# Down-weight chunk transfers of a cross-attention and FFN kernel moved from SyncE's to ScalarE's instruction stream

## The chip, the core and the metric

One core of one Trainium2 chip runs the whole program. The metric is the device time of one launch in microseconds, the median of 3 runs. TensorE (PE) multiplies, VectorE (DVE), ScalarE (ACT) and GpSimd (POOL) work on elements, and SyncE (SP) computes nothing: before the change it issues every transfer of the kernel.

## The reference

```python
x = x + xattn(layernorm(x), ctx, Wq, Wk, Wv, Wo)      # 32 heads, 4 key/value heads, head size 128
h = layernorm(x)                                       # 8 x 112 rows of 1024
hid = relu(h @ up_w) ** 2                              # 1024 -> 2048
shared = hid @ down_w                                  # 2048 -> 1024
routed = ((h @ fc1_w) @ expert_w * sum(top2(h @ gate_w))) @ fc2_w
x = x + layernorm(shared + routed, gamma, beta)
```

Everything is float32. The change touches only how parts of `down_w` are prepared while `h @ up_w` is computed.

## The kernel before

**Arithmetic.** The matrix products are done with seven block products in place of eight (Strassen's scheme in Winograd's form), so sums of weight blocks are needed beside the blocks. Every float32 operand is split into a rounded part ("hi", written by ACT with a copy) and the rest ("lo", a subtraction on POOL or DVE), and each product is three matmuls (L2289, L2290, L2291: hi*hi, lo*hi, hi*lo).

**The up stage.** `h @ up_w` runs over 8 pairs of 128-column blocks of the weights, `p` = 0 to 7, and in each pair over 7 products, `n` = 0 to 6. A unit is one product, `u = 7 * p + n`, written here (p,n). One unit is 4 steps of 3 matmuls over 448 rows. Between the units of pair 0 TensorE also does the last 7 routed products. For each pair four weight blocks of 128x512 (called A11, A21, A22, A12, 256 KB each, in `slab_raw`) are loaded by `load_up` (L926). POOL makes four sums of them (`up_sum`, L1186; the first needs A21 and A22, and overwrites A21), and for n = 0, 1, 2, 3 and 6 the lo parts (`up_lo`, L1195), in the order sum 1, lo 0, sum 2, lo 1, lo 2, sum 3, sum 4, lo 3, lo 6. ACT makes all the hi parts (`up_hi`, L1524), DVE the lo parts for n = 4 and 5 (L2094). DVE combines each product into the running sums (`up_combine`, L2087), and ACT takes the finished block through Relu (L1535) and Square (L1537) into the hidden rows (`hidden_block`, for n = 2, 4, 5, 6). At n = 0 ACT copies the first product out of its bank (L1613).

**The chunks.** The down products, which come after the up stage, need sums of blocks of `down_w` too. They are made ahead of time in 16 chunks, c0 to c15. Each chunk is two loads of 256 KB (`load_chunk`, L940), four subtractions of 128x256 on DVE (`down_sums`, L2105), and one store of 512 KB to a scratch tensor in DRAM (`store_chunk`, L945). Four buffers are used: X and Z in `act_region_unrounded`, Y in `tile_region`, V in `small_region_unrounded`. The table `CHUNKS` says in which unit DVE makes the sums and in which buffer. c0 to c15 have their sums in (1,0) Y, (1,1) X, (1,3) Z, (1,4) V, (1,6) Y, (2,0) X, (2,3) Z, (2,4) V, (2,6) X, (3,0) Y, (3,3) Z, (3,5) X, (3,6) Y, (4,4) X, (4,6) Y and (5,5) Y.

**What sets the order of the transfers.** SP's list is written out by hand, unit by unit. In units n = 2, 3, 4 and 5 of each pair it waits until A11, A21, A22 or A12 of this pair has been used up and loads the block of the next pair: A11 behind POOL's lo 3, A21 behind DVE's lo part for n = 4, A22 behind DVE's lo part for n = 5, A12 behind POOL's lo 6. In unit (0,4) it loads c0 and in (0,5) c1 to c3. After that the rule is: two units behind the sums of a chunk comes its store (behind a wait for the fourth sum), and five units behind them the load of the next chunk in the same buffer (behind a wait for the store to have landed):

```python
for c in range(len(CHUNKS)):
    if CHUNK_UNIT[c] + 2 == u:
        store_chunk(c)
    later = [i for i in range(c + 1, len(CHUNKS)) if CHUNK_BUF[i] == CHUNK_BUF[c]][:1]
    if CHUNK_UNIT[c] + 5 == u:
        for i in later:
            load_chunk(i)
```

So c4 is loaded in (1,5) for its sums in (1,6), c5 in (1,6) for (2,0), c8 in (2,5) for (2,6), c11 in (3,4) for (3,5), c12 in (3,5) for (3,6), c13 in (4,3) for (4,4).

**ACT's list in the up stage** goes by the same units. In unit u it waits for the product and copies it if n = 0, then makes the hi part of unit u + 3 (in pair 0: u + 2, and two of them, (1,0) and (1,1), in (0,5)), and then does the hidden block, if the unit has one. The hi part of (p+1,1) thus comes in unit (p,5), in front of that unit's Relu, and it waits for POOL's sum 2 of pair p+1.

Of the kernel before, what the change touches and what calls it, by code (L numbers as in the profile page):

```python
# [11 lines left out]
P = 128  # L12
B, SQ, HID = 8, 112, 1024
SC = 375
NH, NKV, D = 32, 4, 128
# [197 lines left out]
def xattn_ffn(nc, x, ctxT, slabs, wkv, gate, gamma, beta, out):  # L213
    with ExitStack() as top:
# [440 lines left out]
        def _(sp):  # L655
# [272 lines left out]
            def down_base(kh):  # L928
                return slab_no(P_FFN) + NK + 2 * NK * kh

            def load_chunk(c):


                buf, use, m, kp = CHUNK_BUF[c], CHUNK_USE[c], c % 4, c // 4
                if use:
                    sp.wait_ge(s_cst[buf], 16 * use)
                to = CHUNK[buf].rearrange("p (e k c) -> p e k c", e=2, k=2)
                for kh in range(2):
                    blocks = slabs[down_base(kh):down_base(kh) + NK].rearrange("(e m) p c -> p e m c", e=2)
                    sp.dma_start(to[:, :, kh, :], blocks[:, :, m, 2 * P * kp:2 * P * (kp + 1)]).then_inc(s_cld[buf], 16)  # L940

            def store_chunk(c):
                buf, use, m, kp = CHUNK_BUF[c], CHUNK_USE[c], c % 4, c // 4
                sp.wait_ge(s_csum[buf], 4 * (use + 1))
                sp.dma_start(td_d[:, kp, :, m, :].rearrange("t p c -> p t c"),  # L945
                             CHUNK[buf].rearrange("p (t c) -> p t c", t=4)).then_inc(s_cst[buf], 16)

            def load_down(d):

                if d >= 2:  # L950
# [11 lines left out]
            for p in range(F_PAIRS):  # L962
                more = p + 1 < F_PAIRS
                for n in range(7):
                    u = 7 * p + n
                    if more and n == 2:
                        sp.wait_ge(s_ulo, lo_count(p, 3))
                        load_up(p + 1, "A11")
                    if more and n == 3:
                        sp.wait_ge(s_ulo2, 2 * p + 1)  # L970
                        load_up(p + 1, "A21")
                    if more and n == 4:
                        sp.wait_ge(s_ulo2, 2 * p + 2)
                        load_up(p + 1, "A22")
                    if more and n == 5:
                        sp.wait_ge(s_ulo, lo_count(p, 6))
                        load_up(p + 1, "A12")
                    if p == 0 and n == 4:
                        sp.wait_ge(s_ftlo, 4)
                        load_chunk(0)  # L980
                    if p == 0 and n == 5:
                        sp.wait_ge(s_mm, C_FFN + RT)
                        for c in range(1, 4):
                            load_chunk(c)
                    for c in range(len(CHUNKS)):
                        if CHUNK_UNIT[c] + 2 == u:
                            store_chunk(c)
                        later = [i for i in range(c + 1, len(CHUNKS)) if CHUNK_BUF[i] == CHUNK_BUF[c]][:1]
                        if CHUNK_UNIT[c] + 5 == u:
                            for i in later:  # L990
                                load_chunk(i)
            sp.wait_ge(s_ulo, lo_count(F_PAIRS - 1, 3))
            sp.wait_ge(s_ulo2, 2 * F_PAIRS - 1)
            load_down(0)
# [229 lines left out]
        def _(act):  # L1224
# [301 lines left out]
            def hidden_block(p, n, i):  # L1526
# [9 lines left out]
                act.wait_ge(s_relu, 4 * p + i + 1)  # L1536
                act.activation(to, to, ACT.Square).then_inc(s_sq, 1)  # L1537

            def down_hi(d):

                act.wait_ge(s_draw[d % 2], 16 * (d // 2 + 1))
                if d == 0:
                    act.wait_ge(s_up, UNITS - 3)
                elif d < 3:
                    act.wait_ge(s_up, UNITS - 2)
                elif d == 3:
                    act.wait_ge(s_up, UNITS)
                elif d == 24:
                    act.wait_ge(s_olo, 4 * 6)
                else:  # L1550
                    act.wait_ge(s_dmm, slab_done(d - 4 if d < 24 else d - 5))
                act.activation(d_slot(d)[0], RAWS[d % 2], ACT.Copy).then_inc(s_dhi, 1)
# [54 lines left out]
            for p in range(F_PAIRS):  # L1607
                last = p == F_PAIRS - 1
                for n in range(7):
                    u = 7 * p + n  # L1610
                    if n == 0:
                        act.wait_ge(s_up, u + 1)
                        act.activation(F_FIRST, UB[0][:, 0:HALF], ACT.Copy).then_inc(s_first_p, 1)  # L1613
                    for v in (u + 2,) if u < 5 else (7, 8) if u == 5 else (u + 3,):
                        if v < UNITS:
                            up_hi(v // 7, v % 7)
                    if p == 0 and n == 2:
                        act.wait_ge(s_mm, C_FFN + 4)
                        row_block_hi("T4", 9)
                    if last and n == 5:  # L1620
                        chunk_hi(0, 0)
                        chunk_hi(0, 1)
                    if n in F_TILES:
                        hidden_block(p, n, list(F_TILES).index(n))
                    if last and n == 5:
                        down_hi(0)
# [1166 lines left out]
```

## Time and profile before

| what | value |
|---|---|
| time, median of 3 runs | 1735.61 us (1735.61 to 1735.88) |
| the profiled execution, its own time | 1735.55 us |
| its span in the trace | 1733.8 us |
| granted TensorE clock, mean | 0.998 |
| TensorE matmul busy | 1705.7 us, 98% of the span |
| VectorE, ScalarE, GpSimd busy | 1026.1, 736.5, 961.6 us |
| up stage with chunk work (about) | 1440 to 1560 us from the span's start |

Times in the rows are microseconds from the span's start. SPq is SP's list of transfers: its durations are those of issuing, not of moving the data. A bracket at the end of a row says how long the engine had been idle before it, and what released it.

### The profile page before, as it was taken

The page shows a single profiled execution, that of the slowest core. Times are in us where ns is not written, and L with a number is a line of the kernel's source. Part 1 is how long each engine was busy: PE and PEld are TensorE (multiplying, and loading weights), DVE is VectorE, ACT ScalarE, POOL GpSimd, SP SyncE. Part 2 cuts the span into 40 slices and gives each one's busy share as a digit, 9 for nine tenths or more (in the row PEclk, how much of TensorE's full clock was granted, in tenths as well). Part 3 has the DMA queues.
Part 4 walks back from the last instruction along what each step waited for, and adds up shares of the span by engine and source line. Part 5 has one row for each costly group of instructions (what it writes and reads, how often), then busy time and mean ns, then how long its engine had stood idle before and what let it go on. Part 6 is the DMA issues. An engine that isn't in the chain of part 4 may idle for free.

```text
span 1733.8 us, 24758 instructions
## 1 busy us (share of the span) xinstructions
PE 1705.7 (98%) x8539; PEld 1502.7 (87%) x8539; DVE 1026.1 (59%) x1520; ACT 736.5 (42%) x1409; POOL 961.6 (55%) x775
## 2 busy tenths in 40 slices
PE   9999999999999999999999999999999999889998
PEld 8988998899999988888988898889888987777887
DVE  3711112743434458875877577757657366866998
ACT  3311212233434357734773477247513224445342
POOL 2365553445555549875767576736534244555565
PEclk9999999999999999999999999999999999999999
DMA  8788876566677669834763476334223105643344
GB/s 271 227 285 284 295 246 214 171 195 219 207 225 247 218 208 303 290 121 142 249 219 121 149 243 211 116 102 152 82 81 113 55 31 175 220 147 97 133 145 158
DMA packets 214295, 319.37 MB, mean 184 GB/s; under 512 B 20304, under 2 KB 174416, under 8 KB 213328
## 3 DMA queue, kind: packets, MB, share of 16 engines
q1 hardware_dynamic: 214224, 318.49, 56.6%
q8 instruction: 37, 0.61, 0.1%
q14 instruction: 34, 0.28, 0.1%
HBM read 211.78 MB, written 106.66 MB: 184 GB/s over the span
## 4 chain that ended last, share of the span: by engine, by line
PE 90%; DVE 3%; POOL 3%; DMA 2%; issue 1%; ACT 1%; SPq 0%; DVEq 0%; POOLq 0%; ACTq 0%
PE bank L2289 28%; PE bank L2290 28%; PE bank L2291 28%; PE bank L2513 5%; POOL slab_raw L1186 1%; DMA slab_raw<-in_slabs 1%; PE bank L2375 1%; POOL tile_region_rounded L1195 1%; DVE act_region_unrounded L2105 1%; POOL act_region L1195 0%; DMA mid_region<-k_latents_scratch 0%; DVE tile_region L2105 0%; PE bank L2654 0%; PE bank L2361 0%; DVE slab_split_unrounded L2125 0%
## 5 line engine op out<-in xcount | busy, mean ns | idle before, releaser
L1102 POOL TENSOR_TENSOR tile_region<-tile_region,small 128x487 f32<-128x487 f32 x224 | 221.1, 1024 | 73.2 <-DVE small L1787 73.1
L2289 PE MATMUL bank<-mid_region 125*128 125x448 f32 (+4 forms) x608 | 248.3, 408 | 0.5 <-DMA mid_region<-k_latents_scratch 0.3
L2290 PE MATMUL bank<-mid_region 125*128 125x448 f32 (+4 forms) x608 | 229.4, 377 | 0.0
L2291 PE MATMUL bank<-mid_region 128*128 128x488 f32 (+4 forms) x572 | 215.0, 376 | 0.0
L2289 PE MATMUL bank<-mid_region,act_region 128*125 128x512 f32 (+3 forms) x434 | 168.5, 388 | 1.7 <-POOL act_region L1195 1.7
L2290 PE MATMUL bank<-mid_region,act_region 128*125 128x512 f32 (+3 forms) x434 | 168.3, 388 | 0.0
L1372 ACT ACTIVATE tile_region<-bank,small 128x487 f32<-128x487 f32 x224 | 153.8, 687 | 30.3 <-DVE small L1791 30.3
L1068 POOL TENSOR_TENSOR slab_raw<-slab_raw 128x256 f32<-128x256 f32 x128 | 98.4, 771 | 120.0 <-DMA slab_raw<-in_slabs 112.5
L1404 ACT ACTIVATE mid_region<-bank 125x512 fp32r<-125x512 f32 x224 | 136.7, 613 | 54.7 <-PE bank L2513 54.7
L1791 DVE TENSOR_REDUCE small<-bank 128x1 f32<-128x487 f32 x224 | 146.0, 653 | 20.8 <-PE bank L2291 20.8
L1842 DVE TENSOR_TENSOR mid_region<-bank,mid_region 125x512 fp32r<-125x512 f32 x224 | 151.8, 683 | 9.3 <-ACT mid_region L1404 9.3
L2291 PE MATMUL bank<-mid_region,act_region 128*125 128x512 f32 (+3 forms) x404 | 156.3, 387 | 0.0
L2513 PEld LDWEIGHTS bank<-ident,tile_region 128*125 128x125 f32 x896 | 131.4, 187 | 15.5 <-POOL tile_region L1102 1.6
L1086 POOL TENSOR_TENSOR slab_split<-slab_raw,slab_split 128x512 fp32r<-128x512 f32 x64 | 87.6, 1371 | 94.3 <-ACT slab_split L1322 94.2
L2513 PE MATMUL bank<-ident,tile_region 128*125 128x128 f32 x896 | 134.4, 273 | 0.8 <-DVE mid_region L1842 0.8
L2291 PE MATMUL bank<-act_region,mid_region 128*128 128x376 f32 (+3 forms) x366 | 128.5, 351 | 0.0
L2289 PEld LDWEIGHTS bank<-mid_region 128*128 128x128 f32 (+2 forms) x608 | 114.7, 189 | 13.8 <-issue 2.7
L2290 PEld LDWEIGHTS bank<-mid_region 128*128 128x128 f32 (+2 forms) x608 | 115.4, 190 | 9.6
L2291 PEld LDWEIGHTS bank<-mid_region 128*128 128x128 f32 (+2 forms) x572 | 107.5, 188 | 14.9
L1662 DVE TENSOR_TENSOR small_region<-bank,small_region 128x375 fp32r<-128x375 f32 (+1 forms) x40 | 22.4, 563 | 164.7 <-ACT small_region L1238 164.6
L1923 DVE TENSOR_TENSOR y_region<-y_region,bank 128x512 f32<-128x512 f32 x105 | 68.8, 682 | 83.0 <-PE bank L2291 82.2
L2289 PE MATMUL bank<-act_region,mid_region 128*128 128x376 f32 (+3 forms) x330 | 115.0, 348 | 0.0
(310 smaller groups left out, 4290.7 us busy)
## 6 DMA issues: line engine op xcount, KB each, us to landing
slab_raw<-in_slabs SPq DMA_DIRECT2D x112, 256.0 KB, 3.8
q_scratch<-y_region SPq DMA_DIRECT2D x16, 1792.0 KB, 8.1
mid_region<-q_scratch SPq DMA_DIRECT2D x32, 896.0 KB, 7.1
slab_raw<-in_slabs SPq DMA_DIRECT2D x48, 512.0 KB, 3.5
weight_sums_scratch<-slab_raw SPq DMA_DIRECT2D x32, 512.0 KB, 4.4
small_region_unrounded<-in_slabs SPq DMA_DIRECT2D x52, 256.0 KB, 4.8
v_scratch<-slab_split SPq DMA_DIRECT2D x8, 1536.0 KB, 7.7
slab_raw<-weight_sums_scratch SPq DMA_DIRECT2D x48, 256.0 KB, 4.5
```

The costliest lines, as they stand in the source:

```text
L1068: pool.tensor_tensor(out, a, b, op).then_inc(s_sum[h], 1)
L1086: pool.tensor_tensor(WB[n][1], WRAW[n], f32(WB[n][0]), ALU.subtract).then_inc(s_blo, 1)
L1102: pool.tensor_tensor(PR[i][:, 0:KEYS], PR[i][:, 0:KEYS], rrow[:, i:i + 1].broadcast_to([P, KEYS]), ALU.mult).then_inc(s_pn, 1)
L1372: act.activation(PR[i][:, 0:KEYS], SB[RING[i]][:, 0:KEYS], ACT.Exp, bias=negmax[:, i:i + 1], accum_out=rowsum[:, i:i + 1]).then_inc(s_exp, 1)
L1404: act.activation(PT[0][0:KT, :, i * P:(i + 1) * P], TB[RING[i]][0:KT, :].rearrange("p (t n) -> p t n", t=4), ACT.Copy).then_inc(s_pth, 1)
L1791: dve.reduce_max(negmax[:, i:i + 1], SB[RING[i]][:, 0:KEYS], AX.X, negate=True).then_inc(s_max, 1)
L1842: dve.tensor_tensor(PT[1][0:KT, :, cols], TB[RING[i]][0:KT, :].rearrange("p (t n) -> p t n", t=4), f32(PT[0][0:KT, :, cols]), ALU.subtract ...
L1923: return dve.tensor_tensor(Y[:, r, cols_of(eh)], Y[:, r, cols_of(eh)], GB[i][:, :], op)
L2289: pe.matmul(out_ap, w[0], a[0], start=first, stop=False)
L2290: pe.matmul(out_ap, w[1], a[0], start=False, stop=False)
L2291: return pe.matmul(out_ap, w[0], a[1], start=False, stop=last)
L2513: last = pe.transpose(TB[RING[i]][0:KT, t * P:(t + 1) * P], PR[i][:, t * KT:(t + 1) * KT], ident[:, :])
```

## The change

`load_chunk` and `store_chunk` move, with their waits, from SP's list to ACT's, and so 32 loads and 16 stores are issued by ACT. They stand in the same units, in ACT's list behind the unit's hi part and ahead of its hidden block. Sizes, buffers, semaphores and the order of the chunks stay. SP keeps `load_up` and everything else. `chunk_base` gives the same number as `down_base`.

```diff
 # SP's list
-                    if p == 0 and n == 4:
-                        sp.wait_ge(s_ftlo, 4)
-                        load_chunk(0)
-                    if p == 0 and n == 5:
-                        sp.wait_ge(s_mm, C_FFN + RT)
-                        for c in range(1, 4):
-                            load_chunk(c)
-                    for c in range(len(CHUNKS)):
-                        if CHUNK_UNIT[c] + 2 == u:
-                            store_chunk(c)
-                        later = [i for i in range(c + 1, len(CHUNKS)) if CHUNK_BUF[i] == CHUNK_BUF[c]][:1]
-                        if CHUNK_UNIT[c] + 5 == u:
-                            for i in later:
-                                load_chunk(i)
 # ACT's list
+            def load_chunk(c):
+                buf, use, m, kp = CHUNK_BUF[c], CHUNK_USE[c], c % 4, c // 4
+                if use:
+                    act.wait_ge(s_cst[buf], 16 * use)
+                to = CHUNK[buf].rearrange("p (e k c) -> p e k c", e=2, k=2)
+                for kh in range(2):
+                    blocks = slabs[chunk_base(kh):chunk_base(kh) + NK].rearrange("(e m) p c -> p e m c", e=2)
+                    act.dma_start(to[:, :, kh, :], blocks[:, :, m, 2 * P * kp:2 * P * (kp + 1)]).then_inc(s_cld[buf], 16)
+            def store_chunk(c):
+                buf, use, m, kp = CHUNK_BUF[c], CHUNK_USE[c], c % 4, c // 4
+                act.wait_ge(s_csum[buf], 4 * (use + 1))
+                act.dma_start(td_d[:, kp, :, m, :].rearrange("t p c -> p t c"),
+                             CHUNK[buf].rearrange("p (t c) -> p t c", t=4)).then_inc(s_cst[buf], 16)
...
                     for v in (u + 2,) if u < 5 else (7, 8) if u == 5 else (u + 3,):
                         if v < UNITS:
                             up_hi(v // 7, v % 7)
                     if p == 0 and n == 2:
                         act.wait_ge(s_mm, C_FFN + 4)
                         row_block_hi("T4", 9)
+                    if p == 0 and n == 4:
+                        act.wait_ge(s_ftlo, 4)
+                        load_chunk(0)
+                    if p == 0 and n == 5:
+                        act.wait_ge(s_mm, C_FFN + RT)
+                        for c in range(1, 4):
+                            load_chunk(c)
+                    for c in range(len(CHUNKS)):
+                        if CHUNK_UNIT[c] + 2 == u:
+                            store_chunk(c)
+                        later = [i for i in range(c + 1, len(CHUNKS)) if CHUNK_BUF[i] == CHUNK_BUF[c]][:1]
+                        if CHUNK_UNIT[c] + 5 == u:
+                            for i in later:
+                                load_chunk(i)
...
                     if n in F_TILES:
                         hidden_block(p, n, list(F_TILES).index(n))
```

## Rows read from the trace of the kernel before

**Rows 1.** The page's first part: busy time, share of the span and instructions.

```profile
PE 1705.7 (98%) x8539; PEld 1502.7 (87%) x8539; DVE 1026.1 (59%) x1520; ACT 736.5 (42%) x1409; POOL 961.6 (55%) x775
```

**Rows 2.** Busy time by stretch: us, PE, PEld, DVE, ACT, POOL, PEclk, DMA share, GB/s.

```profile
1404.00:1440.00 36.00, 36.00 (x166) 30.95 (x166) 20.76 (x21) 8.73 (x12) 12.92 (x8) 1.00 0.09 27
1440.00:1560.00 120.00, 105.48 (x502) 92.78 (x501) 90.41 (x117) 52.88 (x95) 71.02 (x54) 1.00 0.60 189
1560.00:1580.00 20.00, 20.00 (x99) 18.16 (x99) 7.10 (x11) 9.79 (x17) 12.91 (x10) 1.00 0.17 55
```

**Rows 3.** The chain that ended last, 1440 to 1557: start us, us, what.

```profile
1480.48 5.80 DMA slab_raw<-in_slabs
1520.53 5.65 DMA slab_raw<-in_slabs
1540.67 3.83 DMA slab_raw<-in_slabs
```

**Rows 4.** Who waited for what, POOL, 1440 to 1560: us, times, longest.

```profile
POOL slab_raw L1186 <- DMA slab_raw<-in_slabs: 10.9, 5, 3.4
```

**Rows 5.** L926 (`load_up`) by source, 1430 to 1560: issue ns min/median/max; landing.

```profile
L926 SPq DMA_DIRECT2D slab_raw<-in_slabs x26: 327/341/698, 1430.3 to 1558.9; - x26
...
DMA to landing us min/median/max: 2.4/3.2/6.4
```

**Rows 6.** SP's timeline: start us, us, what it issued.

```profile
1441.87 1.90 SPq L940 DMA_DIRECT2D act_region_unrounded<-in_slabs  x4
1443.82 0.98 SPq L940 DMA_DIRECT2D small_region_unrounded<-in_slabs  x2
...
1477.86 0.94 SPq L940 DMA_DIRECT2D small_region_unrounded<-in_slabs  x2
1478.85 0.47 SPq L945 DMA_DIRECT2D down_weight_sums_scratch<-act_region_unrounded  x1
1479.36 1.82 SPq L926 DMA_DIRECT2D slab_raw<-in_slabs  x2
```

**Rows 7.** ACT's timeline in units (0,5), (0,6), (1,5), (1,6) and (2,5).

```profile
1447.77 0.63 ACT L1524 ACTIVATE tile_region_rounded<-slab_raw 128x512 fp32r<-128x512 f32 x1 [2.77 <-POOL slab_raw L1186]
1448.31 0.56 ACT L1535 ACTIVATE slab_split_unrounded<-tile_region 128x448 f32<-128x448 f32 x1
...
1449.39 0.61 ACT L1524 ACTIVATE act_region<-slab_raw 128x512 fp32r<-128x512 f32 x1
...
1468.58 0.63 ACT L1524 ACTIVATE act_region<-slab_raw 128x512 fp32r<-128x512 f32 x1 [3.90 <-POOL slab_raw L1186]
...
1470.48 0.61 ACT L1524 ACTIVATE slab_split<-slab_raw 128x512 fp32r<-128x512 f32 x1
...
1490.44 0.63 ACT L1524 ACTIVATE slab_split<-slab_raw 128x512 fp32r<-128x512 f32 x1 [4.97 <-POOL slab_raw L1186]
```

**Rows 8.** POOL's timeline: lo (1,2), then sum 1 of pair 2, which waits for A22.

```profile
1450.08 1.31 POOL L1195 TENSOR_TENSOR act_region<-slab_raw,act_region 128x512 fp32r<-128x512 f32 x1 [0.31 <-ACT act_region L1524]
...
1464.41 1.29 POOL L1186 TENSOR_TENSOR slab_raw<-slab_raw 128x512 f32<-128x512 f32 x1 [2.23 <-DMA slab_raw<-in_slabs]
```

**Rows 9.** TensorE's timeline: the first matmul of (1,3), which waited for lo (1,3).

```profile
1456.31 0.47 PE L2289 MATMUL bank<-act_region,slab_split 128*128 128x448 f32 x1 [1.20 <-POOL tile_region_rounded L1195]
```

**Rows 10.** DVE's timeline: combine (0,6), sums of c3, c4 and c8.

```profile
1448.90 0.62 DVE L2087 TENSOR_TENSOR tile_region<-y_region,bank 128x448 f32<-128x448 f32 x1 [3.92 <-ACT slab_split_unrounded L1535]
...
1464.09 4.73 DVE L2105 TENSOR_TENSOR small_region_unrounded<-small_region_unrounded 128x256 f32<-128x256 f32 x4
...
1470.54 3.75 DVE L2105 TENSOR_TENSOR tile_region<-tile_region 128x256 f32<-128x256 f32 x4
...
1492.11 5.07 DVE L2105 TENSOR_TENSOR act_region_unrounded<-act_region_unrounded 128x256 f32<-128x256 f32 x4
```

**Rows 11.** L2105 (`down_sums`), 1440 to 1560: ns of one, min/median/max.

```profile
L2105 DVE TENSOR_TENSOR act_region_unrounded<-act_region_unrounded x32: 413/426/1569, 1456.7 to 1527.9; 128x256 f32<-128x256 f32 x32
```

**Rows 12.** L940 (`load_chunk`), 1430 to 1560: us from issue to landing.

```profile
DMA to landing us min/median/max: 2.9/4.5/7.0
```

More of the change, by code:

```diff
@@ L929, in down_base @@
                 return slab_no(P_FFN) + NK + 2 * NK * kh
[L931 to L946, printed above, removed]
             def load_down(d):
@@ L1537, in hidden_block, with chunk_base @@
                 act.activation(to, to, ACT.Square).then_inc(s_sq, 1)
+            def chunk_base(kh):
+                return T_WO + (NKV - 1) * NK + P_FFN - P_SEG2 + NK + 2 * NK * kh
+            def load_chunk(c):
[11 more added lines that the diff above has]
+                             CHUNK[buf].rearrange("p (t c) -> p t c", t=4)).then_inc(s_cst[buf], 16)
             def down_hi(d):
```

## The prediction

> **What bounds the kernel now.** I read the page's busy times first: TensorE is busy 1705.7 us of 1733.8, so 98% of the span is its own work [rows 1], and only the rest can move. The busy time by stretch says where that rest lies for this change. From 1404 to 1440 us and from 1560 to 1580 us TensorE has no gap; from 1440 to 1560, just where the chunks are handled, it is busy 105.48 of 120 us [rows 2], so it idles 14.5 us. The other engines are far from full there too (VectorE 90.41, GpSimd 71.02, ScalarE 52.88), which means a chain from engine to engine and not one full engine. The chain that ended last shows its links that are transfers: three loads of weight blocks, 5.80, 5.65 and 3.83 us long [rows 3]. The waits say the same: GpSimd's first sum of a pair waited 5 times for such a load, 10.9 us in all [rows 4]. The shortest landing of these loads is 2.4 us and the median 3.2 [rows 5], so the long ones stood behind something. SP's timeline shows it: at 1477.86 two chunk loads, at 1478.85 a chunk store, 1 MB together, and then at 1479.36 and just after it A21 and A22 of pair 3, all in one queue [rows 6].
>
> A pair's loop is: VectorE's lo part of (p,5) frees A22, SP loads the next A22, GpSimd makes sum 1, lo 0 and sum 2, ScalarE the hi part of (p+1,1), GpSimd the lo parts and sums 3 and 4, and so on. VectorE reaches that lo part late because its list is filled with chunk sums.
>
> **The change part by part.** All sums are made against the profiled execution, 1735.55 us (a span of 1733.8 and 1.75 around it); the median is 1735.61, so what I add to one holds for the other.
>
> *Taken off SP:* 32 loads and 16 stores of 0.37 to 0.49 us each to issue, and SP's waits for VectorE's sums. By itself this is worth little: A21 and A22 are issued behind VectorE's lo parts, and SP is mostly there in time. What is worth something is that A22 no longer stands behind up to 1 MB of chunk data.
>
> *Put on ScalarE, unit (0,5): +2.4 us.* Six loads (c1 to c3) now stand between the hi part of (1,1), started at 1447.77, and the Relu of (0,5), started at 1448.31 [rows 7]. On SP the same six took 1.90 + 0.98 = 2.88 us to issue [rows 6]. ScalarE can issue while its last copy is still running, so I put the start at about 1447.85, the end at 1450.7, and the Relu 2.4 us later than now. Behind it in ScalarE's list is the hi part of (1,2) at 1449.39, and behind that POOL's lo (1,2), which starts 0.31 us after its previous work, released by ScalarE [rows 8]; then sums 3 and 4, lo (1,3) and the first matmul of (1,3) at 1456.31, which already waits 1.20 for it [rows 9]. VectorE's combine of (0,6) had waited 3.92 us for that same Relu [rows 10], so its list moves by 2.4 too. Nothing in this chain has slack, so all 2.4 arrive.
> The price of an issue on ScalarE isn't in the trace. The nearest rows are SP's: at least 0.33, at most 0.70 us [rows 5]. With 0.33 the term is 2.0 - 0.46 = 1.5, with 0.70 it is 4.2 - 0.46 = 3.7. I take 0.48, since those rows are of the very same loads. A gain is excluded, since ScalarE has only more to do here.
>
> *Pair 1 to 2: -1.1 us.* Ahead of A22 of pair 2 two stores leave the queue. Sum 1 waited 2.23 us for it [rows 8], and I put the landing 1.9 us earlier. The sums of c3 take 4.73 us [rows 10]: one subtraction takes 0.43 alone [rows 11] and 1.2 to 1.3 on average when GpSimd works beside it (a fourth of 4.73 and 5.07 [rows 10]). With GpSimd 1.9 us earlier, one of its pauses falls into c3, which becomes about 1 us shorter, and the Relu of (1,5) and the hi part of (2,2), at 1470.48 [rows 7], come 1.1 earlier. The load of c4 now waits behind hi (2,1), but this comes earlier too: landing about 1470.5 (1468.58 [rows 7] - 1.9 + 0.5 for the first issue + 3.3), VectorE wants it at 1470.54 [rows 10]. Cover: none to spare.
>
> *Pair 2 to 3: -0.1 us.* A22 takes 5.80 us [rows 3]. With two queues sharing the engines I put it at 4.3, and 0.6 is kept from the pair before, so sum 1 and hi (3,1) come 2.1 earlier. But three issues (two loads for c8, one store of c6) now stand between hi (3,1), 1490.44 now [rows 7], and the next Relu and hi part: 3 x 0.48 less the half microsecond that overlaps, about 1.0, and no more than about 1.1 is kept at (3,3), nearly all of it from the pair before. The load of c8 is issued behind hi (3,1), not ahead of it: 1490.44 - 2.1 + 0.9 of issuing + 3.3 = 1492.5 (3.3 between a chunk load's shortest landing, 2.9, and its median, 4.5 [rows 12]), where VectorE now starts at 1492.11 [rows 10]. Even there it would lose little, since late sums meet less of GpSimd.
>
> *Pair 3 to 4: +0.3 us,* by the same three issues (c12, c10) against about 0.9 from A22. *Pair 4 to 5: -1.1 us.* Here A22 takes 5.65 us [rows 3] because the two loads of c13 are issued just ahead of it. They move behind hi (4,6), and I put A22 at 3.2 us, the median [rows 5]. Of those 2.5 us the sums of c13, which must be done before the Relu of (4,5), let only 1.1 through. *Pair 5 to 6: -0.5 us,* of 3.83 against 3.2 [rows 3, 5]. From 1560 us on TensorE's own work sets the pace again [rows 2], and the shift is passed on whole.
>
> *Stores, at nothing.* A store waits for VectorE's sums two units back, and behind it ScalarE's Relu needs a later VectorE result anyway, which covers the wait. If that cover is gone, the hi part behind it is late by the rest of the sums. The wait for a store's landing ahead of a load covers itself in the same way.
>
> Sum: 2.4 - 1.1 - 0.1 + 0.3 - 1.1 - 0.5 = -0.1 us, so **1735.5 us**: two effects of 2.5 us that cancel.
>
> Bounds of the gains: below nothing none of them reaches by itself, and above they can't be more than the 10.9 us that GpSimd waited [rows 4].
>
> The Trainium skill (DMA: Bandwidth & Descriptors, Queues, rings and completion order) says that SP and ACT each own a row of rings on the same 16 engines, and that an engine alternates between rows packet by packet. By that rule A22, alone in its row, would take half or more of the bandwidth at once, and my 4.3 us would be near the upper end; the trace before has only one such row in use and shows nothing of it.
>
> **The rivals.**
> *Slower: the block lands as late as now.* The engines are shared, 189 GB/s on average in this stretch at a busy share of 0.60 [rows 2], and if the bytes and not their order set the landing, A22 keeps its 4 to 6 us. Then the -2.5 is gone, and three times (pairs 1, 2 and 3) three issues stand behind a hi part that is no earlier, 0.9 each or about 2.7 with the chunk of the next unit landing 2 us after VectorE wants it. Median landing of chunk loads is 4.5 us [rows 12], which speaks for that. 2.4 + 2.7 = 5.1, so 1740.7. It decides from the point where A22 of pair 3 takes more than about 5 us. Against it: the shortest landing is 2.4 [rows 5], and the long ones have chunk data right in front.
> The Trainium skill (DMA: Bandwidth & Descriptors, Issuing engines are not separate DMA queues) bears on this rival and speaks against the change: transfers of all issuers run on the same engines, and spreading them saves only the time of issuing. No run here shows it yet.
>
> *Faster: issuing costs ScalarE nearly nothing on the path,* since its list runs ahead of its arithmetic. Then +2.4 goes to 0 and the 1.0 + 0.9 given back in pairs 2 and 3 stay: -2.5 - 1.9 = -4.4, 1731.1. For it: ScalarE is busy only 52.88 of 120 us there [rows 2]. Against it: six issues in a row are 2.9 us and its queue ahead is one copy of 0.63 [rows 7].
>
> *Nothing moves,* because the chunk data was hidden and its issue falls into ScalarE's waits: 1735.6. Against it are rows 3, 4 and 7.
>
> **How the numbers follow.** The forecast has 0.54, nothing moves 0.05, slower 0.24, faster 0.17. A measurement of this kernel can tell about 0.2%, 3.5 us, from no change. The forecast's own range, with 1.5 to 3.7 for the first term and 1 to 4 for the gains, is 1733 to 1738, all of it within 0.2%, and so same gets 0.59, slower 0.24, faster 0.17. The range takes in both rivals: 1730.5 to 1741.0.
>
> **What the profile of after would show.** Right: SP's list without L940 and L945; 48 issues on ScalarE, 0.4 to 0.5 us each; Relu (0,5) some 3 us behind hi (1,1) in place of 0.54, and TensorE's wait before (1,3) longer than 1.20; GpSimd's waits for blocks down from 10.9 us to 4 or 5, and the link of 5.65 down to about 3; DVE waiting for chunks a few times, under 1 us each; TensorE idle between the end of pair 0 and the end of pair 5 within 3 us of 14.5. Wrong: blocks still landing in over 5 us (slower), or issues of 0.1 us, or that don't delay the Relu (faster), or TensorE's gaps moving outside the up stage.

## The result, and the profile after

| what | before | after |
|---|---|---|
| time, median (6 runs each, same chip) | 1736.19 us | 1746.41 us |
| lowest to highest | 1735.61 to 1737.38 | 1741.80 to 1748.58 |
| the profiled execution, its own time | 1735.55 us | 1747.76 us |
| its span | 1733.8 us | 1745.9 us |
| granted TensorE clock, mean | 0.998 | 0.995 |

The ratio is 1.0054 with an interval of [1.0043, 1.0065], so the change costs 0.54%, 9.4 us. The forecast was 1735.5 us, no change, and even its range ended at 1741.0: it was wrong.

The page of the changed kernel first. The second DMA queue, q10, is ScalarE's, with the 16.78 MB of all the chunks' loads and stores. Transfers make up 3% of the chain that ended last, where it was 2%.

```profile
span 1745.9 us, 24758 instructions
...
PE 1712.7 (98%) x8539; PEld 1507.8 (86%) x8539; DVE 1020.2 (58%) x1520; ACT 736.9 (42%) x1409; POOL 961.1 (55%) x775
...
q10 hardware_dynamic: 17152, 16.78, 3.0%
...
PE 90%; DMA 3%; DVE 2%; POOL 2%; issue 1%; ACT 1%; SPq 0%; ACTq 0%; DVEq 0%; POOLq 0%
```

TensorE does the same work, yet its busy time rose by 7 us against [rows 1], so some matmuls took longer, and the clock is the first thing to look at. The busy time by stretch of the changed kernel (columns as in [rows 2]) shows a slower clock and more idle time: from 1440 to 1580 us TensorE is busy 120.0 of 140 us, against 125.5 before [rows 2], and three stretches have a granted clock of 0.91 where all of before's had 1.00.

```profile
1440.00:1460.00 20.00, 15.83 (x74) 13.32 (x73) 7.96 (x11) 7.88 (x14) 11.61 (x9) 1.00 0.44 140
1460.00:1480.00 20.00, 19.30 (x84) 16.89 (x84) 18.04 (x25) 7.37 (x13) 10.90 (x9) 0.91 0.63 197
1480.00:1500.00 20.00, 14.58 (x63) 13.09 (x64) 12.09 (x21) 7.72 (x14) 7.69 (x8) 0.91 0.69 213
1500.00:1520.00 20.00, 17.46 (x83) 14.92 (x81) 16.94 (x24) 7.30 (x14) 11.43 (x9) 1.00 0.65 209
1520.00:1540.00 20.00, 17.31 (x83) 15.35 (x83) 14.00 (x18) 9.05 (x16) 12.18 (x10) 1.00 0.67 210
1540.00:1560.00 20.00, 17.24 (x74) 14.76 (x73) 10.49 (x16) 9.48 (x17) 10.90 (x9) 0.91 0.42 132
1560.00:1580.00 20.00, 18.26 (x88) 16.00 (x87) 11.68 (x13) 9.36 (x18) 12.05 (x10) 1.00 0.25 80
```

**The first unit.** ScalarE's timeline of unit (0,5), which answers to [rows 7]: the six loads take 2.95 us to issue, and the Relu behind them starts 3.03 us after the hi part where before it was 0.54. The bracket's `issue` says only that the Relu waited for nothing else that the profile shows; the two ACTq rows fill that time, 1449.08 to 1452.05.

```profile
1449.07 0.63 ACT L1493 ACTIVATE tile_region_rounded<-slab_raw 128x512 fp32r<-128x512 f32 x1 [2.77 <-POOL slab_raw L1155]
1449.08 1.94 ACTq L1520 DMA_DIRECT2D act_region_unrounded<-in_slabs  x4
1451.04 1.01 ACTq L1520 DMA_DIRECT2D small_region_unrounded<-in_slabs  x2
1452.10 0.58 ACT L1504 ACTIVATE slab_split_unrounded<-tile_region 128x448 f32<-128x448 f32 x1 [2.40 <-issue]
...
1496.67 0.63 ACT L1493 ACTIVATE slab_split<-slab_raw 128x512 fp32r<-128x512 f32 x1 [4.92 <-POOL slab_raw L1155]
1496.67 0.90 ACTq L1520 DMA_DIRECT2D act_region_unrounded<-in_slabs  x2
1498.13 0.58 ACT L1504 ACTIVATE mid_region_unrounded<-tile_region 128x448 f32<-128x448 f32 x1 [0.84 <-issue]
```

The last three lines are unit (2,5). The load of c8 cannot be issued before the hi part of (3,1), and that one waited 4.92 us for GpSimd. On SP's list nothing held the chunk's load back like this: before, it was issued 5 us ahead of that hi part (1490.44 [rows 7]).

```profile
1485.40 0.88 SPq L940 DMA_DIRECT2D act_region_unrounded<-in_slabs  x2
```

**The loads are in the chain now.** The waits, VectorE's for chunks and GpSimd's for blocks, 1440 to 1572 us. VectorE waited 7.2 us for chunks, in 6 waits, where before it was 0.3. GpSimd's waits for blocks fell only from 10.9 [rows 4] to 8.8, and the longest grew from 3.4 to 5.3.

```profile
DVE act_region_unrounded L2108 <- DMA act_region_unrounded<-in_slabs: 4.4, 3, 1.6
DVE tile_region L2108 <- DMA tile_region<-in_slabs: 2.4, 2, 1.3
DVE small_region_unrounded L2108 <- DMA small_region_unrounded<-in_slabs: 0.4, 1, 0.4
```

```profile
POOL slab_raw L1155 <- DMA slab_raw<-in_slabs: 8.8, 5, 5.3
```

The chain that ended last (start, us, what) is shown below. Before, it had three transfers in it [rows 3], 15.3 us, all of them weight blocks. Now there are seven, 31.3 us, and four of them are chunk loads.

```profile
1475.10 3.90 DMA act_region_unrounded<-in_slabs
...
1485.07 7.60 DMA slab_raw<-in_slabs
1492.81 1.26 POOL slab_raw L1155
1494.07 1.23 POOL act_region L1164
1495.37 1.28 POOL slab_raw L1155
1496.67 0.38 ACT slab_split L1493
1497.08 3.81 DMA act_region_unrounded<-in_slabs
...
1509.79 4.51 DMA slab_raw<-in_slabs
...
1518.84 3.66 DMA tile_region<-in_slabs
...
1529.56 4.05 DMA slab_raw<-in_slabs
...
1555.94 3.77 DMA tile_region<-in_slabs
```

Read it as a loop, for it is most of the loss: A22 lands, GpSimd makes sum 1, lo 0 and sum 2, ScalarE begins the hi part, and only then is the load of c8 issued; it lands 3.81 us later, VectorE makes c8's sums, the combines and the lo part that frees A22, and the next A22 is issued. Before, the chunk was loaded while GpSimd worked; now the loop holds two transfers in series where it had one.

**TensorE behind its gaps.** Its timeline at the first product of (1,3). It waited 2.11 us, made five steps from matmul to matmul of 0.20 to 0.31 us, and then nine steps of 0.37 us, from 1461.32 until 1464.68: the lower of its two levels, 1.2 in place of 2.4 GHz.

```profile
1460.18 0.47 PE L2292 MATMUL bank<-act_region,slab_split 128*128 128x448 f32 x1 [2.11 <-POOL tile_region_rounded L1164]
1460.49 0.36 PE L2293 MATMUL bank<-act_region,tile_region_rounded 128*128 128x448 f32 x1
...
1461.69 0.57 PE L2292 MATMUL bank<-act_region,slab_split 128*128 128x448 f32 x1
1462.07 0.57 PE L2293 MATMUL bank<-act_region,tile_region_rounded 128*128 128x448 f32 x1
...
1464.68 0.37 PE L2294 MATMUL bank<-mid_region,tile_region_rounded 128*128 128x448 f32 x1
```

Such a stretch is about nine matmuls at 0.37 in place of 0.20, so it loses 1.5 us. There are three of them between 1440 and 1580, from 1461.3, 1495.9 and 1550.0, each behind a gap of 2.1 to 3.3 us; before had none there, and one at 1588, where the down products start.

**Where the 12.1 us between the two profiled spans are.** 1.3 us were there at the hi part of (1,1) (1449.07 against 1447.77 [rows 7]): TensorE was busy 1438.55 us up to 1441.3, 1.35 more than before up to 1440, for the same 7296 matmuls, so it is not the change's. TensorE's idle time from 1440 to 1580 grew from 14.5 to 20.0, which is 5.5, and three slow stretches are 4.5. Together 11.3. The rest is not located: the same 600 matmuls are busy 131.30 us from 1441.3 to 1592.6 where before it was 125.48 from 1440 to 1580, 5.8 more, of which the slow stretches explain 4.5. By the medians and the ratio the change itself costs 9.4 to 10.2.

ScalarE copies the first product of each pair out of its bank, which makes good mileposts. Start of that copy of pair 1 to 7 before, and by how much later it is in other kernels (one profiled execution of each, so about a microsecond is no difference):

```
pair                       1        2        3        4        5        6        7
before, us             1450.98  1472.09  1493.65  1514.04  1533.70  1552.77  1569.94
after                    +3.8     +5.2     +7.2     +8.6     +9.6    +14.6    +12.5
e8, first loads on ACT   +3.1     +3.2     +3.6     +3.8     +3.4     +4.7     +3.0
e5, late loads on SP     +0.2     +0.6     +4.3     +6.0     +7.2    +10.0     +7.8
e2, stores on ACT        +0.2     -0.5     +0.3     +0.5     +0.9     +1.4     +1.4
f1, retimed on SP        -0.1     -0.8     -1.5     -1.2     -2.4     -0.2     -2.0
```

### The profile page after: what moved, and what is told of

Read it like the earlier page. It is cut to its first block, busy times and chain, and to the rows that moved or that the text cites. A ratio compares the mean times of both kernels' runs of the same rounds, so it can differ in the third digit from the quotient of the medians.

```text
span 1745.9 us, 24758 instructions
## 1 busy us (share of the span) xinstructions
PE 1712.7 (98%) x8539; PEld 1507.8 (86%) x8539; DVE 1020.2 (58%) x1520; ACT 736.9 (42%) x1409; POOL 961.1 (55%) x775
## 3 DMA queue, kind: packets, MB, share of 16 engines
q10 hardware_dynamic: 17152, 16.78, 3.0%
## 4 chain that ended last, share of the span: by engine, by line
PE 90%; DMA 3%; DVE 2%; POOL 2%; issue 1%; ACT 1%; SPq 0%; ACTq 0%; DVEq 0%; POOLq 0%
PE bank L2292 28%; PE bank L2293 27%; PE bank L2294 27%; PE bank L2516 5%; DMA slab_raw<-in_slabs 1%; PE bank L2378 1%; DMA mid_region<-k_latents_scratch 1%; POOL slab_raw L1155 1%; DVE tile_region L2108 1%; POOL tile_region_rounded L1164 1%; DMA act_region_unrounded<-in_slabs 0%; DMA tile_region<-in_slabs 0%; DVE act_region_unrounded L2108 0%; POOL act_region L1164 0%; PE bank L2657 0%
```

## The experiments

The theory after the result: the loads of c4 to c15 come late, because ScalarE's list holds them back until the hi part in front of them can run; the rest is the time of issuing. The rivals: that the second queue itself slows the blocks, that the issuing alone is the price, and that TensorE's clock is.

Each ratio is against the kernel before, run beside the experiment. Its medians were 1736.44 us for e1 to e4, 1737.51 for e5 to e8 and 1736.74 for f1 to f3, so ratios are to be compared, and not medians. The code below shows the lines that matter; functions and waits that move with them are left out.

**e1: c0 to c3 are loaded by SP again.**

```diff
 # SP's list, in (0,4) and (0,5)
+                        load_chunk(0)                  # sp.dma_start
...
+                        for c in range(1, 4): load_chunk(c)
 # ACT's list
-                        load_chunk(0)
...
-                        for c in range(1, 4): load_chunk(c)
```

> The loads of c0 to c3 go back to SP, and everything else stays on ScalarE. Theory A (six issues ahead of the Relu of (0,5) put 2.6 us on a chain without slack): 2.6 us faster than the changed kernel, the first matmul of (1,3) back near 1456.3, and probably no fall of the TensorE clock at 1461, which gives about 1.5 more: 1742 to 1744 us. Theory B (the loss is all in chunk loads that come late and in blocks that land late, pairs 2 to 5): no change, 1746 us.

Measured: 1743.82 us (1742.38 to 1744.78), ratio 1.0040 [1.0027, 1.0053]. TensorE's first matmul of (1,3) is back to 1456.98 and waits 1.48 us:

```profile
1456.98 0.47 PE L2309 MATMUL bank<-act_region,slab_split 128*128 128x448 f32 x1 [1.48 <-POOL tile_region_rounded L1188]
```

VectorE's waits for chunks are 8.4 us, and A22 of pair 3 takes 7.22. The trace shows that the term of unit (0,5) is real. By the ratios some three quarters of the loss are elsewhere, but the interval overlaps that of the change. As expected there is no slow stretch at 1461, but e1 has three too, the first at 1477.9, so nothing was saved there.

**e2: stores alone on ScalarE. e3: loads alone on ScalarE.**

```diff
 # e2, ACT's list: only the stores of the change
                         if CHUNK_UNIT[c] + 2 == u:
                             store_chunk(c)             # act.dma_start; load_chunk stays on SP
 # e3, ACT's list: only the loads of the change
                         if CHUNK_UNIT[c] + 5 == u:
                             for i in later:
                                 load_chunk(i)          # act.dma_start; store_chunk stays on SP
```

> Only the 16 stores are issued by ScalarE, all loads by SP. Theory A and the late-load theory: none of their causes is left, so 1736 us or a little under it, with A22 of pair 3 landing in 4 to 5 us. Theory C (a second queue takes the bandwidth from the weight blocks): A22 of pair 3 still takes over 6 us and the time stays above 1739.

> Only the 32 loads are issued by ScalarE, the stores by SP. Issue and lateness of the loads as the cause: the whole loss stays, 1745 to 1747 us, with VectorE waiting about 7 us for chunks. If the stores on ScalarE cost something themselves: 1740 to 1743.

Measured: e2 1736.51 us, ratio 1.0000 [0.9991, 1.0009]; e3 1744.93 us, ratio 1.0042 [1.0030, 1.0055]. The waits of e2 and then of e3:

```profile
DVE act_region_unrounded L2126 <- DMA act_region_unrounded<-in_slabs: 0.7, 1, 0.7
...
POOL slab_raw L1184 <- DMA slab_raw<-in_slabs: 10.0, 5, 3.3
```

```profile
DVE act_region_unrounded L2126 <- DMA act_region_unrounded<-in_slabs: 5.3, 3, 2.2
DVE tile_region L2126 <- DMA tile_region<-in_slabs: 4.4, 3, 2.1
...
POOL slab_raw L1175 <- DMA slab_raw<-in_slabs: 10.2, 5, 3.2
```

The loads are the loss. The stores cost nothing, as forecast, but they gain nothing either: with half of the chunk data on the other queue GpSimd still waits 10.0 us for blocks. A22 of pair 3 takes 6.40 us in place of 5.80 [rows 3], and not the 4 to 5 that was expected. So a second queue with stores in it costs no time; what one with loads does to a block's landing is not shown by this run. In e3 A22 of pair 3 took only 5.55 us, and the loss was there all the same: it does not hang on that block alone.

**e4: the change, with 35 matmuls more.** Five unused matmuls ahead of the first product of seven units, so that TensorE works in its gaps; their result is never read.

```diff
+                if (p, n) in ((1, 2), (1, 3), (2, 3), (3, 0), (3, 3), (4, 3), (5, 3)):
+                    pe.wait_ge(s_ev, C_FFN + 4)
+                    for k in range(5):
+                        pe.matmul(bank[6][:, 0:HALF], F11[0][:, k % 4, 0:P], F11[0][:, k % 4, :], start=True, stop=True)
```

> The changed kernel, with 5 matmuls of 448 columns whose result is not used in each of the seven longest gaps of TensorE in the up stage ((1,2), (1,3), (2,3), (3,0), (3,3), (4,3), (5,3)), about 1.0 us a gap. Theory D (part of the loss is TensorE at 1.2 GHz behind a gap, three stretches of about 3.4 us at 0.37 us a matmul in place of 0.21): the stretches go away and the time falls by 3 to 4.5 us, to 1742 to 1743. If the clock costs nothing because TensorE is starved anyway: 1746 or up to 1 us more.

Measured: 1744.29 us (1741.96 to 1745.14), ratio 1.0039 [1.0026, 1.0052]. In the profiled execution one of the three slow stretches is left, and the mean clock is 0.997. That is 2 us less than after, for two stretches of 1.5 us each, and less than the 3 to 4.5 that were expected; the two intervals overlap, so a gain is not shown. The clock is at any rate not the most of the loss: 7 us stay with TensorE kept at work.

**e5: everything on SP, but the loads as late as in the change.** The kernel before, with one wait more ahead of each load of c4 to c15, for the hi part that stands in front of it in ScalarE's list. ScalarE issues nothing.

```diff
                             for i in later:
+                                sp.wait_ge(s_uhi, u + 4)
                                 load_chunk(i)
```

> The kernel before, all transfers on SP, but SP waits ahead of each load of c4 to c15 for the hi part that ScalarE makes in that unit, so the chunks are as late as in the changed kernel and ScalarE issues nothing. Late theory (the loads come late because they stand behind a hi part that waits for GpSimd; VectorE then waits for them and frees the next A22 late): 1742 to 1744, VectorE waiting 6 to 8 us for chunks. Issue theory (the issues hold up ScalarE between a hi part and its Relu): 1736 to 1738.

Measured: 1743.59 us, ratio 1.0033 [1.0021, 1.0045]. One line of code, one queue, and 60% of the loss. The waits and the chain of e5:

```profile
DVE act_region_unrounded L2106 <- DMA act_region_unrounded<-in_slabs: 6.9, 3, 3.3
DVE tile_region L2106 <- DMA tile_region<-in_slabs: 6.0, 3, 2.4
...
POOL slab_raw L1187 <- DMA slab_raw<-in_slabs: 14.3, 6, 5.8
```

```profile
1482.63 7.73 DMA slab_raw<-in_slabs
1495.42 3.99 DMA act_region_unrounded<-in_slabs
```

Even A22 of pair 3 takes 7.73 us, as in the change (7.60), though there is only one queue. Its waits are longer than those of after (12.9 against 7.2 us for chunks), probably because here a waiting load also holds back the blocks behind it in SP's list (GpSimd waits 14.3 us for them, against 8.8). That makes 0.33% a price of lateness and of held-back blocks together. Late loads, with nothing issued by ScalarE, are enough for most of the loss; how much of it the held-back blocks are is not separated.

**e6: the issues alone.** The kernel before, and where the change has the 24 loads of c4 to c15 ScalarE issues 24 stores of 64 KB from a constant tile to unused memory (its declaration and SP's last wait are left out below).

```diff
+                        if CHUNK_UNIT[c] + 5 == u:
+                            for i in later:
+                                for h in range(2):
+                                    act.dma_start(idle_d[2 * (i - 4) + h], ident[:, :]).then_inc(s_idle, 16)
```

> The kernel before with 24 more transfers of 64 KB issued by ScalarE, two wherever the changed kernel loads one of c4 to c15; the real loads and stores stay on SP. Their result is not used. Late theory: 1736 to 1738. Issue theory: 1741 to 1744.

Measured: 1738.93 us, ratio 1.0010 [1.0001, 1.0019]. VectorE never waits for a chunk. ScalarE's timeline in unit (2,5) of e6, the same place as above:

```profile
1491.33 0.63 ACT L1527 ACTIVATE slab_split<-slab_raw 128x512 fp32r<-128x512 f32 x1 [5.00 <-POOL slab_raw L1189]
1491.34 0.83 ACTq L1628 DMA_DIRECT2D unused_scratch<-ident  x2
1492.21 0.58 ACT L1538 ACTIVATE mid_region_unrounded<-tile_region 128x448 f32<-128x448 f32 x1 [0.25 <-issue]
```

Two issues of 0.42 us leave ScalarE idle for only 0.25, since the hi part of 0.63 covers the rest; the Relu starts 0.88 behind the hi part, where before it was 0.53. The price includes 1.5 MB of extra data, which the change doesn't have. On the other hand these issues wait for nothing, and single issues of the change took longer, up to 1.27 us.

**e7: the loads of c4 to c15 on ScalarE, but ahead of the unit's hi part.** c0 to c3 on SP, the stores as in the change.

```diff
 # ACT's list, unit u
+                    (the rule for load_chunk)
                     for v in (u + 2,) if u < 5 else (7, 8) if u == 5 else (u + 3,):
                         if v < UNITS:
                             up_hi(v // 7, v % 7)
-                    (the rule for load_chunk)
```

> c0 to c3 loaded by SP, the stores on ScalarE as in the changed kernel, and the loads of c4 to c15 on ScalarE too but ahead of the unit's hi part in place of behind it. Late theory: nearly all of the loss goes, 1736 to 1738, VectorE waiting under 1.5 us for chunks. Issue theory: the issues are still on ScalarE, 1740 to 1743.

Measured: 1740.30 us, ratio 1.0016 [1.0006, 1.0026]. The late theory had expected 1736 to 1738 and waits under 1.5 us, so it missed by itself; the time lies in the range of the issue theory. It is to be read against e1, which differs only in this place: 1.0016 against 1.0040. VectorE's waits for chunks fall from 8.4 to 3.9 us. Two kernels issue the same transfers from the same engine, one place apart, and the place is worth 0.24%, with intervals that just miss each other. What is left holds 3.9 us of waits for chunks, the 24 issues and an A22 of pair 3 of 7.58 us.

**e8: c0 to c3 alone on ScalarE.** The first half of the change's edits, (0,4) and (0,5), and nothing else.

```diff
 # ACT's list: only these (their waits left out)
                     if p == 0 and n == 4: load_chunk(0)
                     if p == 0 and n == 5:
                         for c in range(1, 4): load_chunk(c)
```

> Only the loads of c0 to c3 are issued by ScalarE, all else by SP. Both theories say 2.6 us for the six issues of (0,5), so 1738 to 1740 with the first matmul of (1,3) 2.6 us later; no loss if the 2.6 us are absorbed later on.

Measured: 1739.04 us, ratio 1.0010 [1.0001, 1.0019]. TensorE at (1,3):

```profile
1459.44 0.47 PE L2309 MATMUL bank<-act_region,slab_split 128*128 128x448 f32 x1 [2.10 <-POOL tile_region_rounded L1188]
```

That is the same wait as in after, and 3.1 us later than [rows 9], 0.6 of it already there at the hi part of (1,1) (1448.34). The mileposts show it: +3.1 at pair 1 and nothing added behind it. The time was read at 1.7 us where the trace shows 2.5, within the interval of 0.2 to 3.3. Behind this gap of 2.1 us the matmuls kept their usual steps, unlike those of after.

**f1, f2, f3: can the block's landing be bettered at all?** f1 keeps everything on SP and moves five stores and three loads a unit or more, away from the loads of A22 that had them in front. f2 is the kernel before with five unused matmuls in six units and 14 ahead of the first down product; f3 is both. All their chunks are made and used as before.

```diff
 # f1
+STORE_UNIT = {0: 11, 1: 11, 5: 18, 9: 25, 12: 32}
+LOAD_UNIT = {7: 15, 13: 29, 14: 33}
...
-                        if CHUNK_UNIT[c] + 2 == u:
+                        if STORE_UNIT.get(c, CHUNK_UNIT[c] + 2) == u:
                             store_chunk(c)
...
-                        if CHUNK_UNIT[c] + 5 == u:
-                            for i in later:
+                        for i in later:
+                            if LOAD_UNIT.get(i, CHUNK_UNIT[c] + 5) == u:
                                 load_chunk(i)
```

> The kernel before, all on SP, with chunk transfers moved out of the way of A22: the stores of c0, c1, c5, c9 and c12 behind it in their pair, the loads of c7 and c13 one and two units earlier, that of c14 one later. If the bytes in flight set when a weight block lands (the reading of the runs so far), A22 of pair 3 and pair 5 land in 4 us or less and the time falls by 1 to 3 us against the kernel before. If VectorE's sums set the pace of the pairs whatever A22 does: no change.

> The kernel before with unused matmuls in the gaps of TensorE: five each in (1,3), (2,3), (3,0), (3,3), (4,3), (5,3) and fourteen ahead of the first down product. If a gap of over 3 us is what costs the clock behind it: the stretch of half speed at the start of the down stage goes, 1 to 1.5 us faster. If the clock is lost for another reason, or the fillers cost as much as they save: within 1 us of the kernel before.

> Both together. If their causes are separate, the sum of the two: 2 to 4 us faster than the kernel before.

| kernel | median, us | ratio to before |
|---|---|---|
| f1 | 1734.56 | 0.9988 [0.9978, 0.9999] |
| f2 | 1736.19 | 0.9996 [0.9987, 1.0005] |
| f3 | 1733.77 | 0.9983 [0.9974, 0.9992] |

GpSimd's waits for blocks in f1 (A22 of pair 5 took 3.79 us, where [rows 3] has 5.65; A22 of pair 3 took 5.0 where it was 5.80, and not the 4 that was expected):

```profile
POOL slab_raw L1188 <- DMA slab_raw<-in_slabs: 5.6, 5, 2.6
```

So the aim that a change of this kind can have is reached without a second issuer, by moving transfers in time. It is worth 2 us (0.01 to 0.22%), since half of the saved 5.3 us of waits comes back as waits for chunks (2.8 us where it was 0.3). From 1460 to 1490 us the long links of f1's chain are four chunk stores, 5.2 to 6.2 us each, that the load behind them in SP's list waits for. Unused matmuls alone bring nothing: f2 lost the slow stretch at the start of the down products, and had one at 1470 instead. f3 had none in its profiled execution, at a mean clock of 0.999, and is the fastest kernel here, 3.0 us below before by its median. The difference of f3 to f1 is inside their intervals.

## Why the prediction was wrong, step by step

**Unit (0,5), +2.4: right.** In after (1,3) starts 3.87 us later than [rows 9], 1.3 of it from before, so 2.6. The price taken from SP's rows, 0.48 an issue, is ScalarE's too: 0.37 to 0.49 for most of them. Undone alone (e1) or done alone (e8) it is worth 1.5 to 2.6 us of time, by medians and ratios.

**Stores, at nothing: right,** by e2 (1.0000).

**The gains of the blocks, -2.5 in all over the pairs: wrong.** The steps from milepost to milepost beside the forecast, us:

```
                    forecast    after less before    of it one slow stretch
pair 1 to 2           -1.1           +1.4                  1.5
pair 2 to 3           -0.1           +2.0                  1.5
pair 3 to 4           +0.3           +1.4                   -
pair 4 to 5           -1.1           +1.0                   -
pair 5 to 6           -0.5           +5.0                  1.5
pair 6 to 7             0            -2.0                   -
```

The step that failed first is "Pair 1 to 2". A22 of pair 2 did come as forecast: sum 1 waited 0.21 us for it in place of 2.23 [rows 8], and the sums of c3 took 2.77 us in place of 4.73 [rows 10]. But the sums of c2, which the forecast left out, now lay beside GpSimd's work and grew by the same 2 us. The first row is before, the others are after:

```profile
1460.10 2.81 DVE L2105 TENSOR_TENSOR act_region_unrounded<-act_region_unrounded 128x256 f32<-128x256 f32 x4
1464.71 4.78 DVE L2108 TENSOR_TENSOR act_region_unrounded<-act_region_unrounded 128x256 f32<-128x256 f32 x4
1466.48 1.29 POOL L1155 TENSOR_TENSOR slab_raw<-slab_raw 128x512 f32<-128x512 f32 x1 [0.21 <-DMA slab_raw<-in_slabs]
```

"Pair 2 to 3" failed in two places, and the fault returns in the pairs behind it. A22 "with two queues sharing the engines" was put at 4.3 us and took 7.60. The sentence behind it, "Even there it would lose little, since late sums meet less of GpSimd", put at nothing what e5 measured as 0.33% and e7 against e1 as 0.24%.

The second place weighs more. Side by side, in one profiled execution of each:

```
                               ratio    DVE waits    POOL waits    A22 of pair 3
                                        for chunks   for blocks
before                           -         0.3          10.9           5.80
e2, stores on ACT              1.0000      0.7          10.0           6.40
e8, first loads on ACT         1.0010      0.7          10.4           6.17
e6, issues only                1.0010      0             9.4           5.94
e7, loads ahead of hi          1.0016      3.9          11.3           7.58
e5, late loads on SP           1.0033     12.9          14.3           7.73
e1, all but the first loads    1.0040      8.4           8.0           7.22
e3, loads on ACT               1.0042      9.7          10.2           5.55
after                          1.0054      7.2           8.8           7.60
```

All kernels that lose 0.3% or more wait over 7 us for chunks, and none of the others does. A22 of pair 3 does not sort them so: e7 has it late and loses little, e3 has it early and loses much. By pair, GpSimd's waits for A22 were 2.23, 3.45, 1.47, 2.88 and 0.83 us for pairs 2 to 6 before, and 0.21, 5.25, 2.16, 0.99 and 0.23 after. So the blocks did gain in three of five pairs, and the time did not follow.

On A22: the forecast saw what stands in front of it in the queue, and took that away. But the data doesn't go away. From 1480.15 to 1485.1 us the changed kernel issued 2.75 MB (c6, c7, the stores of c4 and c5, A11, A21, A22), and all of it shared the engines: A11, 2.6 us to land before, took 7.5, A21 7.9, A22 7.60. The store of c5, issued 1.6 us ahead of A22, took 10.0 and landed 0.8 us behind it. So the second queue did let A22 pass one store, and that was worth less than what the crowd cost. The DMA engines had no time to spare in this stretch, 0.99 busy (columns as in [rows 2]):

```profile
1485.00:1490.00 5.00, 5.00 (x27) 4.63 (x26) 4.34 (x9) 1.54 (x4) 1.29 (x1) 1.00 0.99 283
```

At 283 GB/s the 2.75 MB need some 10 us by my estimate. What the second queue by itself does to a block's landing stays open: with loads as late as in the change, A22 took 7.73 in one queue (e5) and 5.55 with the loads on ScalarE and the stores on SP (e3).

The Trainium skill (DMA: Bandwidth & Descriptors, Issuing engines are not separate DMA queues) says that transfers of all issuers run on the same engines and that spreading them saves only issuing time. The runs agree: 1.0000 for e2. Its section Queues, rings and completion order lets an engine alternate between rows; the overtaken store fits that, but A22, alone with its pair's blocks in its row, was slower than in one common row (7.60 against 5.80; in e3, with the stores in its row, 5.55).

On the chunk: the forecast had the load of c8 at 1488.3 and its landing at 1492.5, 0.4 us behind VectorE's start. In the trace it was issued at 1496.67, landed at 1500.9, and VectorE had been waiting 1.55 us. It was late because the hi part ahead of it waits for A22, so a late block makes a late chunk, and a late chunk makes the next block late. The prediction costed the wait that this list adds for one chunk and one pair, and each as slack or no slack. It is a loop: from c8 on VectorE waited 1.1 to 1.6 us for each of c8, c11, c12, c13 and c15. With the slow stretches taken off, the steps behind pair 2 are 0.5, 1.4, 1.0 and 3.5 us. The last has c15's load in it (wait 1.1 us), and 2 us of it come back in the next pair.

**TensorE's clock** stood nowhere in the prediction. Three slow stretches are about 4.5 us of the profiled 12.1. Filling the gaps gave 2 us back by the medians (e4), within overlapping intervals.

**The rival "slower"** came nearest: its turning point, A22 of pair 3 above 5 us, was passed, and it had the chunk landing after VectorE wants it. But the block was as late as before or later only in pairs 3 and 4. Its price of 5.1 us was half of what came, since it too took the late chunk for three single delays. Of the signs listed, those of the issuing held (Relu 3 us behind the hi part, a wait over 1.20 ahead of (1,3)), and those of the gain didn't: GpSimd's waits 8.8 in place of 4 to 5, the link of 5.65 at 4.05 in place of 3, VectorE's six waits 1.2 us on average in place of under 1, TensorE idle 20.0 in place of 14.5 plus or minus 3.

**The parts, each measured alone:** late loads 0.33% (e5), 24 issues on ScalarE 0.10% (e6), six first loads 0.10% (e8), stores 0.00% (e2). Their sum of 0.53% matches the 0.54% of the change. With intervals of about 0.1% to each side, held-back blocks in e5 and extra data in e6, that match is partly luck; by e7 against e1 lateness is 0.24%. What is shown is the order: late loads first, issuing second, stores nothing.

Open stays how much of the loss the clock is on average, since executions of one kernel differ in their slow stretches, and how much of the lateness would be left if ScalarE issued at no price; no run was made on that.

## What to carry to other kernels

A prefetch must not stand behind a wait of the work that it is meant to run ahead of: before a transfer is moved to another engine's list, look up what each instruction in front of it waits for, and follow that wait round the loop to the transfer's own user. A second issuing engine takes nothing out of the data in flight; moving the other transfers in time (f1) brought a little, 2 us. And a change with an expected gain and an expected loss is best run in its halves, here stores and loads, since one of them was free and the other was the whole result.

## What the runs showed of the hardware that was not expected

- A load of 256 KB took 2.6 us to land before and 7.5 us after, though in neither was a transfer issued just ahead of it in its own queue (A11 of pair 3). In after it lay within 2.75 MB issued in 5 us from two engines.
- Issuing is not always 0.4 us. Around 1482 us, while SP was issuing too, single issues took longer: this is the source view of the chunk loads in after (ns, min/median/max), where one of V's loads took 1272. SP alone had one of 1451 before, so it isn't the second issuer as such; the cause is not shown.

```profile
L1520 ACTq DMA_DIRECT2D small_region_unrounded<-in_slabs x4: 432/491/1272, 1451.0 to 1482.2; - x4
```

- TensorE's granted clock fell behind some gaps and not behind others as long: in after it fell behind those that ended at 1460.18, 1495.43 and 1548.70 (2.11, 3.33 and 2.11 us), and not behind those that ended at 1482.09 and 1527.91 (2.11 and 2.13 us). It fell 0.5 to 1.3 us after work had begun again and stayed down for eight or nine matmuls, some 3 us. The stretches of 0.37 us a matmul in e1, e2, e3, e6, f1 and f2 look the same; in e5, behind a gap of 4.41 us, there were twelve.
